# A five-stage attention and mixture-of-experts kernel: VectorE's linked chains divided into steps, six small operations left out, and new orders

## Time and profile before

| | |
|---|---|
| median of 3 runs | 1278.15 us (1277.8 to 1279.9) |
| the profiled execution | 1278.19 us |
| its span | 1276.3 us |
| TensorE (PE) busy | 1156.3 us, 10338 matmuls |
| VectorE (DVE) busy | 1044.5 us, 2837 instructions |
| ScalarE (ACT) busy | 865.6 us |
| GpSimd (POOL) busy | 699.2 us |
| mean granted TensorE clock | 0.951 |

### The profile page before, as it was taken

One profiled execution on the slowest core, in us unless ns is written; L12 is line 12 of the kernel. 1 busy time (PEld: TensorE's weight loads), 2 busy tenths in 40 slices (PEclk: granted clock), 3 DMA queues, 4 the chain that ended last, 5 costly groups with the idle time before them and its releaser, 6 DMA issues.

```text
span 1276.3 us, 27899 instructions
## 1 busy us (share of the span) xinstructions
PE 1156.3 (91%) x10338; PEld 833.9 (65%) x10338; DVE 1044.5 (82%) x2837; ACT 865.6 (68%) x1684; POOL 699.2 (55%) x827
## 2 busy tenths in 40 slices
PE   1567578999999999999999999999999998999998
PEld 1344445675767677676767676776757676766775
DVE  3667877989889898989899898989898898768653
ACT  0335455786868686777868676877868685866665
POOL 3202122666464757566574747566664647455775
PEclk9656879999999999999999999999999999999999
DMA  6000001001010101001010101001010101000000
GB/s 198 21 10 12 12 25 29 17 4 43 10 37 17 38 17 37 18 5 43 10 36 18 37 17 37 18 21 33 4 44 9 38 2 37 17 10 17 10 9 9
DMA packets 63847, 32.69 MB, mean 26 GB/s; under 512 B 29281, under 2 KB 63073, under 8 KB 63329
## 3 DMA queue, kind: packets, MB, share of 16 engines
q1 hardware_dynamic: 61696, 26.83, 8.4%
q10 hardware_dynamic: 2016, 4.08, 0.9%
HBM read 24.73 MB, written 4.19 MB: 23 GB/s over the span
## 4 chain that ended last, share of the span: by engine, by line
PE 78%; DVE 10%; POOL 6%; ACT 3%; issue 2%; DMA 1%; SPq 0%; POOLq 0%; DVEq 0%; ACTq 0%
PE py L697 16%; PE pa L543 5%; PE pa L508 4%; PE pg L687 3%; PE pu L687 3%; PE pg L688 3%; PE pg L689 3%; PE pu L688 3%; PE pu L689 3%; PE pa L532 3%; POOL xn L856 2%; PE pa L550 2%; PE pb L590 2%; PE pb L596 2%; PE pa L697 2%
## 5 line engine op out<-in xcount | busy, mean ns | idle before, releaser
L895 POOL TENSOR_TENSOR moe<-moe 128x512 f32<-128x512 f32 x256 | 331.1, 1295 | 293.3 <-DVE moe L1194 179.0
L697 PE MATMUL py<-wd_s,moe 128*128 128x128 f32 x1856 | 250.7, 280 | 0.2
L697 PEld LDWEIGHTS py<-wd_s,moe 128*128 128x128 f32 x1856 | 232.9, 192 | 19.9 <-issue 4.4
L1073 DVE TENSOR_REDUCE q_st<-pa 128x4 f16<-128x480 f32 x256 | 168.4, 658 | 42.1 <-PE pa L508 40.2
L1194 DVE SCALAR_TENSOR_TENSOR moe<-tg,pg 128x512 f32<-128x512 f32 x232 | 157.8, 680 | 49.0 <-ACT tg L818 46.7
L818 ACT ACTIVATE tg<-pg 128x512 f32<-128x512 f32 x232 | 140.2, 604 | 75.2 <-PE pg L689 74.3
L756 ACT ACTIVATE probs<-pa 120x512 f32<-120x512 f32 x256 | 138.9, 598 | 49.4 <-PE pa L532 46.9
L832 ACT ACTIVATE moe<-pu 128x512 f32<-128x512 f32 x232 | 139.2, 600 | 15.9 <-PE pu L689 13.9
L508 PE MATMUL pa<-kbd,qkht 128*128 128x480 f16 x256 | 101.3, 396 | 24.5 <-DVE q_st L1073 19.5
L856 POOL TENSOR_SCALAR xn<-x,lnm,lnr 128x128 f32<-128x128 f32 x192 | 90.0, 481 | 5.2
L687 PE MATMUL pg<-x4h,wg_h 128*128 128x512 f16 x232 | 88.9, 383 | 3.7 <-DVE moe L1194 0.2
(11 more groups left out here) (200 smaller groups left out, 2743.8 us busy)
## 6 DMA issues: line engine op xcount, KB each, us to landing
xin<-in_x SPq DMA_DIRECT2D x16, 256.0 KB, 2.8
xres<-in_x SPq DMA_DIRECT2D x16, 256.0 KB, 3.0
kbd<-qkht SPq DMA_DIRECT2D x256, 7.5 KB
out_x<-acc SPq DMA_DIRECT2D x16, 256.0 KB, 4.2
ctxt_a<-in_ctx_t SPq DMA_DIRECT2D x16, 240.0 KB, 2.7
ctxt_b<-in_ctx_t SPq DMA_DIRECT2D x16, 240.0 KB, 3.4
ctxn_b<-in_ctx SPq DMA_DIRECT2D x16, 240.0 KB, 4.1
wd_s<-in_wd ACTq DMA_DIRECT2D x1, 1024.0 KB, 8.4
```

The costliest lines, as they stand in the source:

```text
L697: mm = pe.matmul(moe_y(g, e)[:, j, :], hu[:, u % 3, j * S:(j + 1) * S], wd_s[:, u, :], start=(half == 0 and j == 0), stop=(half == 1), ski ...
L895: pool.tensor_tensor(hu[:, u % 3, :], gw[:, u % 3, :], us[:, u % 3, :], ALU.mult)\
L1073: dve.tensor_reduce(q_st[:, t, 4 * c:4 * c + 4, 3 * HD], pa[:, BM, 0:4 * SC].rearrange("p (h k) -> p h k", h=4), AX.X, ALU.max, negate=Tru ...
```

## The change

Three things. (1) VectorE's list of steps is made finer: ln1 to ln4 in two steps, rms in ten, quant in five, the turns, s1 and p1n in two, h2t in three, the gate in five. `link` is divided into `mark` (raise the semaphore) and `meet` (wait for it); a step ends with mark, the next begins with meet, and steps of other stages may stand between. (2) The clip of quant multiplies by 1/127 as well, so its reciprocal is the scale and the clipped value the inverse: two multiplications go. In h2t the same takes away one for each tile (fc2's factor takes what is left). These are six instructions and five links a group (LINKS_B 23 to 18). (3) All strings of TURNS for TensorE, ScalarE, VectorE and GpSimd are new. Products, transfers and ScalarE's and GpSimd's instructions are the same.

```diff
@@ -43,7 +43,7 @@
 MAGIC = 12582912.0
 RSQRT_SEED = 1597463007.0
 WSCALE = 64.0
-LINKS_N, LINKS_A, LINKS_B, LINKS_D = 13, 4, 23, 7
+LINKS_N, LINKS_A, LINKS_B, LINKS_D = 13, 4, 18, 7
 S0, S1, BM, BO, PB = range(5)
...
-        w_steps = ["wabs", "wint", "gate", "wg", "wu"]
+        w_steps = ["wabs", "wint", "gate_w", "wg", "wu"]
         stage_steps = {"w": w_steps, "n": n_steps, "a": a_steps, "b": b_steps, "d": d_steps, "c": c_steps}
 
+        split = {"ln1": ["ln1", "ln1_mv"], "rms": [("rms", i) for i in range(10)], "ln2": ["ln2", "ln2_mv"],
+                 "quant": [("quant", i) for i in range(5)], "ln3": ["ln3", "ln3_mv"], "ln4": ["ln4", "ln4_mv"],
+                 "s1": ["s1", "nmax"], "p1n": ["rl", "p1n"], "gate": [("gate", i) for i in range(5)]}
+        for t in range(GB):
+            split[("turn", t)] = [("rden", t), ("turn", t)]
+            split[("h2t", t)] = [("h2t", t), ("clip", t), ("scale", t)]
+        dve_steps = {stage: [part for step in stage_steps[stage] for part in split.get(step, [step])]
+                     for stage in stage_steps}
+        engine_steps = {"dve": dve_steps, "pe": stage_steps, "act": stage_steps, "pool": stage_steps, "sp": stage_steps}
+
         def run_turns(engine, n, a, b, d, c, do_w, do_n, do_a, do_b, do_d, do_c):
 
+            stage_steps = engine_steps[engine]
             groups = {"w": 0 if n == 1 else None, "n": n, "a": a, "b": b, "d": d, "c": c}
             kind = "".join(stage for stage in groups if groups[stage] is not None)
             do = {"w": do_w, "n": do_n, "a": do_a, "b": do_b, "d": do_d, "c": do_c}
...
-                def link(self, ins):
+                def mark(self, ins):
                     self.k += 1
                     ins.then_inc(self.sig.sem, 1)
+
+                def meet(self):
                     dve.wait_ge(self.sig.sem, self.sig.at(self.g, self.k))
+
+                def link(self, ins):
+                    self.mark(ins)
+                    self.meet()
 
                 def end(self):
                     if self.k != self.sig.per:
@@ -950,26 +970,25 @@
 
             cn, ca, cb, cd, cs = Chain(link_n), Chain(link_a), Chain(link_b), Chain(link_d), Chain(link_s)
 
-            def rsqrt(chain, y, v, root, r):
-
-
-                chain.link(dve.tensor_scalar(y.bitcast(I32), v.bitcast(I32), -0.5, RSQRT_SEED, ALU.mult, ALU.add))
-                chain.link(dve.tensor_tensor(root, v, y, ALU.mult))
-                for last in (False, False, True):
-                    chain.link(dve.scalar_tensor_tensor(out=r, in0=root, scalar=-0.5, in1=y, op0=ALU.mult, op1=ALU.mult))
-                    if not last:
-                        dve.scalar_tensor_tensor(out=root, in0=r, scalar=1.5, in1=root, op0=ALU.add, op1=ALU.mult)
-                    ins = dve.scalar_tensor_tensor(out=y, in0=r, scalar=1.5, in1=y, op0=ALU.add, op1=ALU.mult)
-                    if not last:
-                        chain.link(ins)
-                return ins
-
-            def layernorm(chain, n, src):
-
+            def rsqrt(i, y, v, root, r):
+
+                if i == 0:
+                    return dve.tensor_scalar(y.bitcast(I32), v.bitcast(I32), -0.5, RSQRT_SEED, ALU.mult, ALU.add)
+                if i == 1:
+                    return dve.tensor_tensor(root, v, y, ALU.mult)
+                if i % 2 == 0:
+                    return dve.scalar_tensor_tensor(out=r, in0=root, scalar=-0.5, in1=y, op0=ALU.mult, op1=ALU.mult)
+                if i < 7:
+                    dve.scalar_tensor_tensor(out=root, in0=r, scalar=1.5, in1=root, op0=ALU.add, op1=ALU.mult)
+                return dve.scalar_tensor_tensor(out=y, in0=r, scalar=1.5, in1=y, op0=ALU.add, op1=ALU.mult)
+
+            def statistics(n, src):
 
                 for j in range(GB):
                     ins = dve.bn_stats(stats[:, n, j, :], src[:, j, :])
-                chain.link(ins)
+                return ins
+
+            def moments(n):
...
                     dve.wait_ge(qk_sq.sem, qk_sq.at(g, 1))
                     dve.tensor_reduce(ms[:, 0, :], qsq[:, :, :].rearrange("p t (h d) -> p (t h) d", h=H), AX.X, ALU.add)
                     dve.wait_ge(qk_sq.sem, qk_sq.at(g, 2))
-                    cn.link(dve.tensor_reduce(ms[0:SC, 1, :], ksq[0:SC, :, :].rearrange("p t (h d) -> p (t h) d", h=H),
+                    cn.mark(dve.tensor_reduce(ms[0:SC, 1, :], ksq[0:SC, :, :].rearrange("p t (h d) -> p (t h) d", h=H),
                                               AX.X, ALU.add))
-                    cn.link(dve.tensor_scalar(ms[:, :, :], ms[:, :, :], 1.0 / HD, EPS_RMS, ALU.mult, ALU.add))
-                    cn.link(rsqrt(cn, rr[:, :, :], ms[:, :, :], root[:, :, :], nt[:, :, :]))
+                elif name == "rms":
+                    cn.meet()
+                    if t == 1:
+                        cn.mark(dve.tensor_scalar(ms[:, :, :], ms[:, :, :], 1.0 / HD, EPS_RMS, ALU.mult, ALU.add))
+                    else:
+                        cn.mark(rsqrt(t - 2, rr[:, :, :], ms[:, :, :], root[:, :, :], nt[:, :, :]))
                 elif name == "rms_k":
+                    cn.meet()
                     rk = rr[0:SC, 1, :].unsqueeze(2).broadcast_to([SC, GB * H, HD])
                     gg = gg_s[0:SC, :].unsqueeze(1).broadcast_to([SC, GB * H, HD])
                     k3 = kb[0:SC, :, :].rearrange("p t (h d) -> p (t h) d", h=H)
@@ -1073,10 +1099,13 @@
                     dve.tensor_reduce(q_st[:, t, 4 * c:4 * c + 4, 3 * HD],
                                       pa[:, BM, 0:4 * SC].rearrange("p (h k) -> p h k", h=4), AX.X, ALU.max,
                                       negate=True).then_inc(max_done.sem, 1)
-                elif name == "turn":
+                elif name == "rden":
                     dve.wait_ge(oq_ps.sem, oq_ps.at(g, t + 1))
...
+                    cb.meet()
+                    moments(1).then_inc(ln2_ready.sem, 1)
+                elif name == "quant" and t == 0:
+                    dve.wait_ge(xn2_done.sem, xn2_done.at(g))
+                    cb.mark(dve.tensor_reduce(am1[:, :], xn2[:, :, :], AX.X, ALU.max, apply_absolute_value=True))
                 elif name == "quant":
-                    dve.wait_ge(xn2_done.sem, xn2_done.at(g))
-                    cb.link(dve.tensor_reduce(am1[:, :], xn2[:, :, :], AX.X, ALU.max, apply_absolute_value=True))
-                    cb.link(dve.tensor_scalar(am1[:, :], am1[:, :], CLIP, None, ALU.max))
-                    cb.link(dve.reciprocal(sc1[:, :], am1[:, :]))
-                    dve.tensor_scalar(inv1[:, :], am1[:, :], 1.0 / 127.0, None, ALU.mult)
-                    cb.link(dve.tensor_scalar(sc1[:, :], sc1[:, :], 127.0, None, ALU.mult))
-                    for j in range(GB):
-                        ins = dve.tensor_scalar(xq[:, j, :], xn2[:, j, :], sc1[:, j:j + 1], MAGIC, ALU.mult, ALU.add)
-                    cb.link(ins)
-                    for j in range(GB):
-                        ins = dve.tensor_scalar(xq[:, j, :], xq[:, j, :], MAGIC, inv1[:, j:j + 1], ALU.subtract, ALU.mult)
-                    ins.then_inc(xq_done.sem, 1)
+                    cb.meet()
+                    if t == 1:
+                        cb.mark(dve.tensor_scalar(am1[:, :], am1[:, :], CLIP, 1.0 / 127.0, ALU.max, ALU.mult))
+                    elif t == 2:
+                        cb.mark(dve.reciprocal(sc1[:, :], am1[:, :]))
+                    elif t == 3:
+                        for j in range(GB):
+                            ins = dve.tensor_scalar(xq[:, j, :], xn2[:, j, :], sc1[:, j:j + 1], MAGIC, ALU.mult, ALU.add)
+                        cb.mark(ins)
+                    else:
+                        for j in range(GB):
+                            ins = dve.tensor_scalar(xq[:, j, :], xq[:, j, :], MAGIC, am1[:, j:j + 1],
+                                                    ALU.subtract, ALU.mult)
+                        ins.then_inc(xq_done.sem, 1)
...
                 elif name == "h2t":
                     dve.wait_ge(h2t_ps.sem, h2t_ps.at(g, t + 1))
-                    a, s = am2[:, t:t + 1], sc2[:, t:t + 1]
-                    cb.link(dve.tensor_reduce(a, pb[:, :], AX.X, ALU.max, apply_absolute_value=True))
-                    cb.link(dve.tensor_scalar(a, a, 0.5, CLIP, ALU.mult, ALU.max))
-                    cb.link(dve.reciprocal(s, a))
-                    dve.tensor_scalar(s, s, 0.5 * 127.0, None, ALU.mult).then_inc(sc2_done.sem, 1)
+                    cb.mark(dve.tensor_reduce(am2[:, t:t + 1], pb[:, :], AX.X, ALU.max, apply_absolute_value=True))
+                elif name == "clip":
+                    cb.meet()
+                    cb.mark(dve.tensor_scalar(am2[:, t:t + 1], am2[:, t:t + 1], 2.0 * CLIP, 1.0 / 127.0, ALU.max, ALU.mult))
+                elif name == "scale":
+                    cb.meet()
+                    dve.reciprocal(sc2[:, t:t + 1], am2[:, t:t + 1]).then_inc(sc2_done.sem, 1)
                 elif name == "fc2":
```

(33 more changed lines are left out.)

114 lines of the change are left out of this document (65 added, 49 removed).

## The result

The changed kernel takes 1266.1 us (median; 1265.7 to 1267.7) where the kernel before takes 1278.2: a ratio of 0.9905, interval 0.9888 to 0.9922, so 12.1 us or 0.95% faster. Forecast were 1271.0, between 1259 and 1282. The profiled execution spans 1264.1, 12.2 less than before.

The account below looks back on a forecast made before the run. TensorE's queue was taken to bound two thirds of the time. From 1278.15 us, periods -4.2, first stretch -0.6, third -1.6 and emptying -0.5 sum to -6.9: 1271.3, said as 1271.0, range 1259 to 1282.

Parts of the forecast that it names:

- The period: Twelve full periods: each 0.35 us shorter from waits at stacks and xit, -4.2 in all, between 0 and -18.4.
- Only 0.28 lies ahead of 583.71: Of VectorE's 2.8 us a period, only quant's 0.28 comes before the next tile's maximum, which TensorE's max11 awaits.
- VectorE's gain: VectorE, each period: 2.8 us less work, 1.1 from left-out operations and 1.7 from split links; by itself no kernel time.
- Full cover: Rival, periods: the maximum is there in time, all 1.53 us a period gained, 1257.1 us; chance 0.17.
- The moved wait: Rival, periods: max11 and the values behind it give all back, start-up gives 0 to -3, 1275 to 1278; chance 0.2.
- Slower by xn4t: Rival, periods: xn4's transposes wait for GpSimd, costing 1.23 us a period, 1286.1; chance 0.18, smaller misses included.
- Second stretch 0: Second start-up stretch: xit ahead of max10 gains at fc11 and loses at stacks1; 0, between +1 and -1.
- First -0.6: First start-up stretch: four of ten rms steps stand ahead of max10, against max11's 0.58 wait; -0.6 us.
- Third -1.6: Third start-up stretch: split rms chain -1.2, one maximum fewer behind xit -0.4; -1.6 us, between 0 and -5.
- the wait for the k blocks: Start-up, at 152.11: TensorE's wait of 2.71 us goes, as k-block transfers leave some 3 us sooner; worth little.
- the wait of the stacks: Third start-up stretch: stacks1's wait of 1.21 us at 183.34 goes with rms split and maxima between; -1.2 us.
- -0.5, some of it for quant: Emptying: of 12.7 us without TensorE some is for quant; -0.5 us, between 0 and -3.

Follow-up runs that it names:

- experiments 1 and 2: 1: kernel before without the six operations, 1274.1 us; changed kernel with them put back, 1273.1. 2: changed kernel with the old periodic order, chains whole there, 1267.9.
- the operations alone: The kernel before with only the six operations of quant and h2t left out, chains whole and all orders old: 1274.1 us, ratio 0.9954.
- the orders alone: The changed kernel with the six operations put back, new orders and split chains kept: 1273.1 us, ratio 0.995.
- the last try: Changed kernel, GpSimd's xres_b behind product u7, VectorE's max10 between ln3's statistics and moments, xl ahead of u3: 1272.0 us, ratio 0.9941.
- the kernel of 1312 us: The changed kernel with VectorE's max10 ahead of ln3's statistics and moments and u3's product behind max11, in the periodic order: 1312.1 us, ratio 1.0253.

## Why the prediction was right, and where it was off

**The period: right.** -0.35 was forecast, -0.31 measured (70.87 to 70.56), with the wait at max11 at 0.73 and none at the stacks. "Only 0.28 lies ahead of 583.71" was the step that decided, and experiments 1 and 2 bear it out: 2.80 of the 3.38 us of eleven periods come with the operations alone. The new order's two covers and its new wait cancel.

**VectorE's gain: right, and worth as little as said.** Forecast were 2.8 a period, measured 2.6 to 2.7. I had 1.1 for the operations (0.74 measured) and 1.7 for the splits. 1.8 came, but 0.6 of it is fc2's factor, which the new order takes away from GpSimd's product and which the sum did not have; at most 1.2 are the splits'. That the total agrees is in part luck. By the rule in the Trainium skill, VectorE: DVE Perf Modes, section The DRAIN you can't avoid, the splits would have freed nothing; these runs speak against that, with up to 1.2 a period.

**The rivals.** Full cover fell for the reason given, ln3 ahead of max10. Its 1.53 a period was too high as well: the period walked was the long one, and with xit 0.29 earlier the others had 1.24 to give. The moved wait came true for the orders alone (0.29 us in eleven periods), but the shorter quant gains beside them. Slower by xn4t did not come: no mark there. Its mechanism, GpSimd being late for want of VectorE's moments, is real though: it is what the last try ran into at xn3.

**Start-up: mis-sized.** I had written that I would be wrong if start-up moved by more than 5. It did: the first product g0 starts at 212.0 instead of 217.4, where 215 was forecast, and from the second transposes of x the gain is 6.1. "Second stretch 0", at most -1, measured -1.86, and that goes with the granted clock, 0.79 for 0.71, which the sum had no term for. "First -0.6" measured -1.68. The max11 wait went as said, and I had not walked qkht's move in that stretch: it now stands where TensorE waited 0.76 for the last maximum of a tile (one mark of that kind fewer). "Third -1.6" measured -2.59, although the step in it was wrong: the wait for the k blocks did not go, it is spread over three matmuls. Nor did the wait of the stacks go, which was -1.2 of the sum: 0.97 is left of 1.21. The gain lies between xit and those stacks (20.15 for 24.56), with 1.47 lost behind them, and by which step was not settled. So the size came near by luck.

**Emptying: mis-sized.** "-0.5, some of it for quant" measured -3.04. 1.9 of it come with the operations alone, and of these 1.7 at one place, where TensorE stayed shorter at 1.2 GHz behind a wait that was 0.2 shorter. The orders alone give 2.3, and beside the operations some 0.9, which is not clear of the scatter. In the changed kernel that wait is gone.

So 4.2 of the 7.2 us forecast were right in place and nearly in size (3.7 came), and the 5 us missing lay in the stretches to which I had given one sentence each. The sum had no term for the clock, which moved single stretches outside the steady state by 1 to 2 us, also between kernels with the same instructions there.

## What to carry to other kernels

A saving on an engine off the bound is worth what it brings ahead of the one instruction that the bound waits for: here 0.28 of 2.7 us a period. Walk the start-up and the emptying as closely as the steady state, since there a saving can fall on the path, and the granted clock moves a stretch by 1 to 2 us. Divided chains with their new orders were worth 5.4 us in the start-up and 0.5 in eleven periods of the steady state. Before moving an operation of VectorE or GpSimd, look at which of VectorE's operations without a PSUM input would start beside a row of GpSimd's without a gap: one maximum moved ahead, with GpSimd's row 0.5 us later, cost 3.7 us a period, 2.1 of it by the clock.

## What was not expected of the hardware

- A VectorE operation on SBUF alone can be held not for one GpSimd operation but for all that is left of a row without a gap: 0.68 became 3.49 and 3.72 at 128x512, behind three operations. Behind one, 0.16 became 1.23 at 128x4. Not every such operation is held: four statistics of ln1 took 0.86 beside the row in the kernel of 1312 us, no longer than any of their kind. The Trainium skill, SBUF — State Buffer, section SBUF: two separate sides, has an exclusive lock held for an instruction; the runs agree and add that the lock goes to GpSimd's next operation if that is ready. From this I had bounded a caught step at 1.27; the bound was too low.
- A gap of 0.22 on GpSimd is enough to be let in; then it is GpSimd's operation that is longer (1.66 for 1.28).
- VectorE's operations that read PSUM were not held in the same places (0.73 and 0.75 for the convolution's taps at 601.5 and 602.3 beside GpSimd's row in the kernel of 1312 us).
- After a wait of 2.40 us TensorE issued for some 6 us at 1.2 GHz, after one of 2.20 for some 3, and after one of 2.21 at the same place, with the second one's instructions, not at all.
